# The shared feed-forward's router part split by tokens, with one more wait on GpSimd and another order of the opening

## The reference

```
mod = silu(c) @ wmod                               # 8 x 6 x 256: sa, ca, ga, sb, cb, gb
ga, gb: sign kept, magnitude raised to at least 0.25
h = layernorm(x) * (1 + ca) + sa
fused = h @ w_kv_a                                 # 192 query, 64 key/value, 64 rope columns
q  = rmsnorm(fused[:192]) @ w_qb                   # 16 heads x (128 + 64 rope)
kv = rmsnorm(fused[192:256]) @ w_kvb               # 16 heads x (128 key + 128 value)
x  = x + ga * (softmax(causal(q_full @ k_full.T / sqrt(192))) @ v) @ w_o
h = layernorm(x) * (1 + cb) + sb
router: softmax(h @ gate_w.T), best 4 of 16 experts, 128 places for each expert
y = sum over experts of gate * (silu(xg @ w_gate) * (xg @ w_up)) @ w_down
x = x + gb * (y + (silu(h @ sw_gate) * (h @ sw_up)) @ sw_down)      # sw_*: 352 columns inside
```

## Time and profile before

| | |
|---|---|
| median of three runs | 1293.26 us |
| the profiled execution | 1287.12 us, its span 1285.3 us |
| TensorE busy | 1193.3 us (93%), weight loads 954.7 us |
| VectorE busy | 848.6 us (66%) |
| ScalarE busy | 667.5 us (52%) |
| GpSimd busy | 279.6 us (22%) |
| chain that ended last | PE 78%, DVE 9%, DMA 5% |

### The profile page before, as it was taken

How to read it: one execution, slowest core, us unless ns; L and a number is a source line. 1 busy time by engine, 2 the same in 40 slices (tenths; PEclk the granted TensorE clock), 3 DMA queues, 4 the chain that set the end, 5 groups by cost and what they waited for, 6 DMA issues and landing times.

```text
span 1285.3 us, 25913 instructions
## 1 busy us (share of the span) xinstructions
PE 1193.3 (93%) x7556; PEld 954.7 (74%) x7556; DVE 848.6 (66%) x2579; ACT 667.5 (52%) x1922; POOL 279.6 (22%) x332
## 2 busy tenths in 40 slices
PE   6699999999999999999999999999999999995874
PEld 4488877887688768887788768886888768882542
DVE  3367757776687668775777668766877677756221
ACT  1367634675367626764477526762577346741220
POOL 1000022211322132212221122113212132202553
PEclk8799999999999999999999999999999999998985
DMA  9510002000010001000100001000100000003762
GB/s 305 139 45 0 0 1 65 3 0 0 16 49 0 0 16 49 0 0 0 45 20 0 0 16 49 0 0 16 49 0 0 0 30 20 0 1 100 213 150 37
DMA packets 48317, 46.17 MB, mean 36 GB/s; under 512 B 10048, under 2 KB 44960, under 8 KB 48296
## 3 DMA queue, kind: packets, MB, share of 16 engines
q1 hardware_dynamic: 29096, 30.90, 8.3%
q0 software_dynamic: 7168, 6.37, 2.8%
q10 hardware_dynamic: 12032, 8.65, 2.3%
HBM read 35.04 MB, written 15.11 MB: 39 GB/s over the span
## 4 chain that ended last, share of the span: by engine, by line
PE 78%; DVE 9%; DMA 5%; issue 3%; ACT 2%; POOL 2%; POOLq 0%; DVEq 0%; SPq 0%; ACTq 0%
PE PS L675 11%; PE PS L696 10%; PE PS L654 7%; PE PS L655 6%; PE PS L656 6%; PE PS L797 6%; DMA out<-x_res,toku 5%; PE PS L640 5%; PE PS L805 3%; PE PS L827 3%; PE PS L788 2%; PE PS L627 2%; PE PS L630 2%; PE PS L631 2%; PE PS L628 2%
## 5 line engine op out<-in xcount | busy, mean ns | idle before, releaser
L973 ACT ACTIVATE probs<-probs,nmax 128x512 f32<-128x512 f32 (+3 forms) x512 | 283.1, 554 | 127.0 <-DVE nmax L1229 123.1
L1229 DVE CUSTOM_DVE_ANT_0 probs<-PS,cmask 128x512 f32<-128x512 f32 (+3 forms) x512 | 229.3, 488 | 101.0 <-PE PS L656 97.9
L538 POOL DMA_INDIRECT tab_dram<-entry,slot x112 | 110.5, 986 | 389.9 <-PE PS L696 368.6
L654 PE MATMUL PS<-kTh,qTh 128*128 128x512 f32 (+3 forms) x512 | 176.9, 345 | 0.6 <-DVE qTl L1260 0.6
L982 ACT ACTIVATE pT<-PS 128x384 f32<-128x384 f32 (+3 forms) x320 | 126.8, 462 | 77.9 <-PE PS L675 77.9
L675 PE MATMUL PS<-ident,probs 128*128 128x128 f32 x1280 | 165.7, 276 | 0.0
L656 PE MATMUL PS<-kTh,qTl 128*128 128x512 f32 (+3 forms) x512 | 165.4, 323 | 0.0
L655 PE MATMUL PS<-kTl,qTh 128*128 128x512 f32 (+3 forms) x512 | 165.4, 323 | 0.0
L696 PE MATMUL PS<-pT,kmat 128*64 128x512 f32 (+3 forms) x1024 | 152.0, 439 | 0.3 <-issue 0.3
L675 PEld LDWEIGHTS PS<-ident,probs 128*128 128x128 f32 x1280 | 142.4, 141 | 10.3 <-issue 7.4
L696 PEld LDWEIGHTS PS<-pT,kmat 128*64 128x64 f32 x1024 | 68.0, 136 | 76.0 <-issue 62.1
(11 more groups left out here) (237 smaller groups left out, 2112.8 us busy)
## 6 DMA issues: line engine op xcount, KB each, us to landing
x_in<-in_x SPq DMA_DIRECT2D x8, 512.0 KB, 5.9
modb<-mod_dram SPq DMA_DIRECT2D x8, 512.0 KB, 5.4
h_dram<-mod_dram SPq DMA_DIRECT2D x1, 4096.0 KB
h_dram<-h SPq DMA_DIRECT2D x8, 512.0 KB, 3.0
out<-base SPq DMA_DIRECT2D x8, 512.0 KB
pT<-in_wo SPq DMA_DIRECT2D x1, 2048.0 KB, 11.7
tab_dram<-entry,slot POOLq DMA_INDIRECT x112
oT<-in_wqnT SPq DMA_DIRECT2D x1, 1536.0 KB, 10.2
```

The costliest lines, as they stand in the source:

```text
L538: pool.indirect_dma_start(tab_dram[:, :], bass.IndirectOffsetOnAxis(ap=slot[:, j:j + 1], axis=0), entry[:, j, :], None, bounds_check=NE * ...
L654: pe.matmul(PS[:, bank, 0:n], qTh[:, h, rows_q], kTh[:, 0:n], start=True, stop=False)
L973: act.activation(probs[:, UO[u]:UO[u] + UW[u]], probs[:, UO[u]:UO[u] + UW[u]], ACT.Exp, scale=-1.0, bias=nmax[:, u:u + 1], accum_out=psums ...
L1229: dve.tensor_tensor_reduce(out=probs[:, UO[u]:UO[u] + UW[u]], in0=PS[:, SBANK[u], 0:UW[u]], in1=cmask[:, S - UW[u]:S], scale=-1.0, scalar= ...
```

## The change

It has three parts.

1. **In every `middle` after a batch.** The part m = 2 of the shared feed-forward, with the router columns, is computed by tokens: `ffn_router(b, 0, ...)` does the 384 tokens of tiles 0 to 2 before `turn_h2_last`, and `ffn_router(b, 1, ...)` the 128 of tile 3 after it. On ScalarE `nope_copy`, which the rope waits for, now stands ahead of `turned_h2_last`. On GpSimd `post` waits for the rope of batch n (`rope_ready`) before it multiplies `h2`; in the last middle there is no such wait.
2. **The opening.** SyncE loads `x_in` ahead of the query weights, and `wkva_sb` ahead of the rope weights. VectorE takes the statistics of `h1` first, then the modulation, and the gates GA and GB last (SyncE waits for `mod_ready` 2 to store them). TensorE turns `h1` in banks 6 and 7 first, then does half of the fold's part k = 0, the modulation's transposes (now bank 3), the other half, and the latent projection; part k = 1 comes behind that, and `absorb_output` behind the first `q_project`. ScalarE and VectorE follow that order (`query_high`, `query_low`).
3. **Evictions of `wvo`.** Of the four copies from PSUM, ScalarE did all, ahead of the copies of the keys; now ScalarE does two and VectorE two, after `nope_copy` and `q_rope`.

The diff, cut to its core:

```diff
@@ SyncE
+            sp.dma_start(x_in[:], rows(xr, 0)).then_inc(x_landed, 16)
             for dst, src in ((wqn_st[:, :, 0:QL], wqnT), (wqn_st[:, :, QL:], wqnT[:, :, P:QL])):
                 sp.dma_start(dst, src.rearrange("h p n -> p h n")).then_inc(wq_in, 16)
             sp.dma_start(wk_st, wkT).then_inc(wq_in, 16)
-            sp.dma_start(x_in[:], rows(xr, 0)).then_inc(x_landed, 16)
+            sp.dma_start(wkva_sb[:], wkva.rearrange("(c p) n -> p c n", p=P)).then_inc(wk_in, 16)
...
-            sp.wait_ge(mod_ready, 1)
+            sp.wait_ge(mod_ready, 2)
@@ GpSimd
                 pool.wait_ge(h2T_ps, 3 * (b + 1))
+                if n is not None:
+                    wait_alone(pool, rope_ready, n * NPAIR + 1)
                 pool.tensor_tensor(h2[:], h2[:], spread(2), ALU.mult).then_inc(h2_scaled, 1)
@@ TensorE
-            pe.wait_ge(wq_in, 3 * 16)
-            pe.wait_ge(mod_read, 1)
-            for k in range(2):
-                if k:
-                    turn_modulation()
-                for h in range(NH):
-                    bank, col = 2 + 2 * k + h // 8, (h % 8) * KL
+            def absorb_query(k, heads):
+                for h in heads:
+                    bank, col = 4 + 2 * k + h // 8, (h % 8) * KL
                     mm = pe.matmul(PS[:, bank, col:col + KL], wqn_st[:, h, bass.ts(k, P)], wk_st[:, h, :],
                                    start=True, stop=True)
-                mm.then_inc(wabs_ps, 1)
+                return mm
...
             def ffn(b, m, banks):
-                wide = w + (NE if m == 2 else 0)
...
+            def ffn_router(b, part, banks):
+                off, w = MT[2]
+                lo, hi = (0, S - P) if part == 0 else (S - P, S)
+                for c in range(2):
+                    pe.wait_ge(h2T_ready, 4 * b + 2 * part + c + 1)
+                    pe.matmul(PS[0:w + NE, banks[0], lo:hi], sg_sb[:, c, off:off + w + NE], h2T[:, c, lo:hi],
+                              start=c == 0, stop=c == 1)
+                    mm = pe.matmul(PS[0:w, banks[1], lo:hi], su_sb[:, c, off:off + w], h2T[:, c, lo:hi],
+                                   start=c == 0, stop=c == 1)
+                return mm
...
                 else:
-                    absorb_output()
-                    pe.wait_ge(wvo_ready, 4)
+                    absorb_query(1, range(NH)).then_inc(wabs_ps, 1)
...
                 if pre:
                     q_project(0, n * NPAIR, (2, 3))
+                if not post:
+                    absorb_output()
                 if post:
+                    pe.wait_ge(x1_ready, 3 * b + 3)
+                    ffn_router(b, 0, (3, 4))
                     pe.wait_ge(n2_ready, 2 * b + 2)
                     turn_h2_last()
-                    ffn(b, 2, (3, 4))
+                    ffn_router(b, 1, (3, 4)).then_inc(gu_ps, 1)
...
-            turn_h1(0, 0)
-            turn_h1(0, 1)
+            pe.wait_ge(const_ready, 3)
+            turn_h1(0, 0, 6)
+            turn_h1(0, 1, 7)
+            pe.wait_ge(wq_in, 3 * 16)
+            absorb_query(0, range(0, NH // 2))
+            turn_modulation()
+            absorb_query(0, range(NH // 2, NH)).then_inc(wabs_ps, 1)
             middle(0, 0, False, True)
@@ ScalarE
                     if not post:
-                        act.wait_ge(wvo_ps, 1)
-                        for a in range(4):
-                            act.activation(wvo[:, 2 * a:2 * a + 2, :]..., PS[:, 4 + a, :], ACT.Copy)
+                        query_high(1)
...
                 if post:
                     turned_h2(b)
-                    turned_h2_last(b)
                 if pre:
                     nope_copy(n * NPAIR)
+                if not post:
+                    act.wait_ge(wvo_ps, 1)
+                    for a in range(2):
+                        act.activation(wvo[:, 2 * a:2 * a + 2, :]..., PS[:, 2 + a, :], ACT.Copy)
                 if post:
+                    turned_h2_last(b)
                     tanh_gate(b, 0, 2, 3)
...
+            turned_h1(0, (6, 7))
+            query_high(0)
@@ VectorE
                 if pre:
                     for k, (low, high, bank, lo) in ...:
+                        if not post and k == 0:
+                            query_low(1)
...
                     for part in q_rope(n * NPAIR):
                         part()
+                if not post:
+                    dve.wait_ge(wvo_ps, 1)
+                    for a in range(2, 4):
+                        dve.tensor_copy(wvo[:, 2 * a:2 * a + 2, :]..., PS[:, 2 + a, :])
...
             h1_statistics(0)
             h1_normed(0)
+            (copy of the modulation, 1 + CA, 1 + CB, mod_ready, modT, mod1, qg_sb, then GA and GB, mod_ready)
+            query_low(0)
```

More of the change, by code:

```diff
@@ L783, in ffn @@
                 off, w = MT[m]
-                wide = w + (NE if m == 2 else 0)
                 for c in range(2):
-                    if m == 2:
-                        pe.wait_ge(h2T_ready, 4 * b + c + 3)
-                    pe.matmul(PS[0:wide, banks[0], :], sg_sb[:, c, off:off + wide], h2T[:, c, :],
+                    pe.matmul(PS[0:w, banks[0], :], sg_sb[:, c, off:off + w], h2T[:, c, :],
                               start=c == 0, stop=c == 1)
@@ L879, in middle @@
                     place()
+                if not post:
+                    pe.wait_ge(wvo_ready, 4)
                 if pre:
@@ L1087, in middle, with query_high @@
                     exps(n * NPAIR, (0, 1, 2))
-            act.wait_ge(gain_ready, 1)
-            for k, (high, pe_st) in enumerate([(wq0h, pe0_st), (wq1hh, pe1_st)]):
+            def query_high(k):
+                high, pe_st = ((wq0h, pe0_st), (wq1hh, pe1_st))[k]
+                act.wait_ge(gain_ready, 1)
                 act.wait_ge(wabs_ps, k + 1)
@@ L1268, in step @@
                 if last and more:
+                    modulation(b + 1)
                     h1_statistics(b + 1)
@@ L1456, in middle @@
                         part()
+                if not post:
+                    dve.wait_ge(wvo_ps, 1)
+                    for a in range(2, 4):
+                        dve.tensor_copy(wvo[:, 2 * a:2 * a + 2, :].rearrange("p a n -> p (a n)"),
+                                        PS[:, 2 + a, :]).then_inc(wvo_ready, 1)
                 if post and pre:
@@ L1493, in _, with query_low @@
             h1_normed(0)
-            for k, (high, low, pe_st) in enumerate([(wq0h, wq0l, pe0_st), (wq1hh, wq1l, pe1_st)]):
+            dve.wait_ge(mod_ps, 1)
+            dve.tensor_copy(midT[0:B].rearrange("b a s -> b (a s)"),
+                            PS[0:B, 0:3, :].rearrange("b a n -> b (a n)")).then_inc(mod_read, 1)
+            dve.wait_ge(mod_read, 1)
+            ch.step(dve.tensor_scalar(mod_sb[:, CA, :], mod_sb[:, CA, :], 1.0, None, ALU.add))
+            dve.tensor_scalar(mod_sb[:, CB, :], mod_sb[:, CB, :], 1.0, None, ALU.add).then_inc(mod_ready, 1)
+            dve.wait_ge(modT_ps, 1)
+            ch.step(dve.tensor_copy(modT[:].rearrange("p k b -> p (k b)"), PS[:, 3, 0:8 * B]))
+            modulation(0)
+            dve.wait_ge(wr_in, 6 * 16)
+            dve.tensor_scalar(qg_sb[:], qg_sb[:], SCALE, None, ALU.mult).then_inc(gain_ready, 1)
+            for k, i in enumerate((GA, GB)):
+                ch.step(dve.tensor_scalar(sgn[:, 0, :], mod_sb[:, i, :], 0.0, 2.0, ALU.is_ge, ALU.mult))
+                ch.step(dve.tensor_scalar(sgn[:, 0, :], sgn[:, 0, :], -1.0, 0.5 if i == GB else 1.0, ALU.add, ALU.mult))
+                ch.step(dve.scalar_tensor_tensor(out=sgn[:, 1, :], in0=mod_sb[:, i, :], scalar=-1.0,
+                                                 in1=mod_sb[:, i, :], op0=ALU.mult, op1=ALU.max))
+                gate = dve.scalar_tensor_tensor(out=mod_sb[:, i, :], in0=sgn[:, 1, :], scalar=0.25,
+                                                in1=sgn[:, 0, :], op0=ALU.max, op1=ALU.mult)
+                if i == GA:
+                    ch.step(gate)
+                else:
+                    gate.then_inc(mod_ready, 1)
+            def query_low(k):
+                high, low, pe_st = ((wq0h, wq0l, pe0_st), (wq1hh, wq1l, pe1_st))[k]
                 for j, (src, lo, hi) in enumerate(((latent_ps(k), 0, KL), (pe_st, KL, P))):
```

53 lines of the change are left out of this document (16 added, 37 removed).

## The result

The changed kernel takes 1255.11 us (median of four runs, 1250.13 to 1256.14) against 1293.22 (four runs, 1292.52 to 1293.86), which is 38.1 us less. The profiled execution took 1254.99 us, its span 1253.1, against 1287.12 and 1285.3 before: 32.1 us by the profiles.

What follows compares the result with a forecast made beforehand. TensorE, busy 93% of the span, was taken as the bound. Seven middles 16.8, the last middle 3.0 and the opening 10.2 summed to 30.0 us, so 1293.26 would become 1263.3, range 1256 to 1273.

Steps and rivals of the forecast that it cites:

- The mechanism of the middles: Seven middles: router matmuls fill idle TensorE time, rope's last step escapes GpSimd's passes; 2.4 us each, 16.8 in all.
- The last middle: Middle without a next batch: part 0 fills TensorE's gap before tile 3's turning; gain 3.0 us, range 2.2 to 3.4.
- The rivals of the middle: Middles: GpSimd stalls other VectorE instructions, 1271, chance 0.08; narrow records dear, 1288, 0.04; GpSimd late, 1298, 0.02.
- Left at nothing: Opening, half clock around the first scores: up to 2 us more gain or a fall elsewhere, counted as zero.
- the term of 10.2 us: Opening: first scores earlier by 12.0 - 0.3 - 1.1 - 0.4 = 10.2 us, range 5 to 13.
- my 24.6: Opening: half fold and modulation's transposes end at 24.6, where the latent projection starts instead of 36.59, 12.0 us earlier.
- my 1.8: Opening, latent projection to first scores: losses of 0.3 for second fold and query copies, 1.1 `absorb_output`, 0.4 `wvo` evictions.
- The clock rival: Opening: latent projection, `absorb_output` and the `q_project` between run at half clock, costing some 7 us: 1270, chance 0.13.

Runs made afterwards that it cites:

- the pair of the first group: Traces of the kernel before, run again unchanged (1286.78 us against 1286.52), and of the kernel before with only the middles' edits (1265.32).
- the middle alone: Kernel before with the router part by tokens, `nope_copy` moved ahead and GpSimd's wait, opening and `wvo` copies as before: 1265.32 us, ratio 0.9833.
- The opening alone: Changed kernel with the three edits of the middle undone, copies of `wvo` still shared: 1271.96 us, ratio 0.9892 to the kernel before.
- the first and third group: Sets of kernels timed together on one chip beside the kernel before, which took 1286.52 us in the first, 1286.37 in the third.
- the split alone: Kernel before with only the router part computed by tokens, old order on ScalarE, no new GpSimd wait: 1310.2 us against 1286.37, ratio 1.0184.

## Why the prediction was wrong by 8 us

**What was right.** The mechanism of the middles, and their sizes. `qtok` at 0.69 us, `q_turn` right behind the 128-column matmuls, those at 0.12 us a record, the wait of 0.55 for ScalarE, GpSimd out of the way. Between its batch's latent projection and itself, `q_turn` stands 2.5 us earlier (26.96 instead of 29.49), where I had 2.4; the batches are 2.2 us shorter in the first pair of profiles and 2.6 in the pair of the first group (139.56 before, 136.98 with the middle alone). All that the edit gives lies between a batch's latent projection and its first scores: 37.4 us in every old middle and 34.85 in every new one, whichever the trace, a difference of 2.57. 7 x 2.57 + 3.1 = 21.1, and the middle alone gave 21.2 for 19.8. The last middle gave 3.1 for 3.0. The rivals of the middle are out: no VectorE or ScalarE instruction beside GpSimd's passes got longer, narrow records aren't dear, and GpSimd is nowhere late (its next work, the mask of the experts, still finds it idle for 11.4 us).

**The step that failed** is the opening's, "Left at nothing" for the clock behind the first scores, and with it the term of 10.2 us. The opening alone is worth 14.6 us by the medians. Five traces have the old opening and seven the new one; their means, with the first pair of profiles in brackets:

```
                             old      new     difference       forecast
to the latent projection    36.62    24.01   -12.6 (-12.9)      -12.0
to the first scores         27.46    28.79    +1.3  (+0.5)       +1.8
to the second batch        101.84    98.47    -3.4  (-3.4)        0
sum                        165.92   151.28   -14.6 (-15.8)      -10.2
```

- To the latent projection. In the profile of the changed kernel the fold started at 18.09 and was over by 22.61, 2 us before my 24.6: it ran at full clock, and the modulation's transposes took 0.59 from their start to the next matmul, instead of 0.95. What was late next was the rope table, landed at 23.57 (I had 23.8), and it kept 1.1 of those 2 us.
- From there to the first scores the losses are there: `absorb_output` 3.63 us, partly in the wait for the rope, and 1.09 us of copies on ScalarE, with a wait before the scores of 1.47 us for 0.56 before. That the means come within 0.5 us of my 1.8 is in part luck, since this stretch took from 25.4 to 30.3 us in the seven new traces, by how much of it was at half clock.
- From the first scores to the second batch I had put nothing, and 3.4 us came. I read the clock to 67.20, the end of the first stretch at half, named "up to 2 us" for it and didn't take it, and left out the next one, from 74.0 to 77.4. That the clock of this stretch is what the 3.4 us are is shown by the table above. What holds it up is shown less well, by one trace each: with `absorb_output` and the copies moved out of the wait for the rope 1.7 of the 3.4 us return, with all four copies on ScalarE 3.0.

Of the 8.2 us that the forecast missed, 4.4 are this term's (14.6 for 10.2) and 1.4 the middles' (21.2 for 19.8; each middle gives 2.57 where I had 2.4).

**The remaining 2.4 us** are not an edit's; they go with the scale on which I read the median. I carried the 6.1 us between the profiled execution (1287.12) and the median before (1293.26) over to the kernel after. There it was 0.1: 1254.99 and 1255.11. From profile to profile I forecast 1257.1, and 1254.99 came, 2.1 off, and that is in part luck: the opening gave 5.6 more than its term and the middles 1.3 more, while the end took 2.1 and the unchanged part of the batches some 2.6 away (102.9 us each, 102.5 before). The kernel before takes 1286.4, 1286.5, 1289.1 or 1293.2 by the group, and the changed one 1252.4, 1252.4 and 1255.1; the first comparison's 38.1 is the largest of three differences. Why the kernel before stood 6 us higher in its first runs isn't known: no trace of such a run exists.

**The clock rival**, at 0.13, foresaw the right quantity with the wrong sign. In the two later traces of the changed kernel half clock covers much of the latent projection and of the query projection, 17 us in all, and the first scores come 3.0 us later than in the first; but it ends before them, and the stretch behind them is at full clock in all three.

**Left open.** Why one execution has 6.8 us of half clock in the opening and another of the same kernel 17; why the clock falls behind the wait of 1.87 us in six traces and not in eight; and why batches of the same code took 137.76, 137.41 and 136.98 us in three traces of the changed kernel. What differs there lies behind a batch's first scores, where no edit reaches: 102.1 us in every trace of the first and third group, 102.5 to 102.7 in the second, 102.5 and 102.9 in the first pair.

## What to carry to other kernels

Three edits of the middle make one: the split alone costs 23.8 us, and with the copy moved ahead of ScalarE's tile 3 it gains, since otherwise it pushes the rope into GpSimd's pass. When an engine's instruction is far over its median in one place, look for what runs beside it, and move that; here one wait gave 11.2 us. And price each gap of TensorE in such an opening twice, for itself and for the clock behind it: read the granted clock over the whole stretch that follows, to the point from which it stays up, before putting that term at nothing. Since single executions differ by 3 us there, one trace doesn't give its size.

## What the runs showed of the hardware

- A wait of 3.88 us in a middle was followed by 6.8 us at half clock, seven times of seven; the middles with 1.33 us there, 21 in three traces (the kernel before, twice, and the opening alone), never had one.
- 7.6 us at half clock behind the first scores cost 3.4 us, a little under half of their length. The same records take up to about twice as long in it (1.94 us for 1.06, 7.03 for 3.68), so half of that time would have been spent at full clock too.
- A wait of 1.87 us in this stretch was followed at once by 3.4 us at half clock in six traces, and by none in eight.
- The fold's second part, 32 records, took 3.68 us at full clock, where the same records took 7.03 at half before.
- A VectorE instruction of 0.69 us with two inputs in SBUF took 2.65 to 2.67 beside GpSimd's multiplication, in every trace in which they met, and 0.69 in every other.
